# Routed results of a mixture-of-experts layer added to token rows in DRAM by indexed accumulating DMAs, in place of gathers at the end

## The reference, cut to what matters

```python
h = _rmsnorm(x, rms_weight)
logits = ht @ router_w
probs = softmax(logits)
topv, topi = top_k(probs, 2)
topv = topv / sum(topv)
eo = (silu(ht @ w_gate[e]) * (ht @ w_up[e])) @ w_down[e]
moe = sum over the two chosen e of topv * eo
sh = silu(ht @ sw_gate) * (ht @ sw_up) @ sw_down
out = x + moe + sh
```

## Time and profile before

| | |
|---|---|
| median of 3 runs | 627.8 us (627.37 to 627.97) |
| profiled execution, its own time | 628.29 us |
| its span, first to last instruction | 626.5 us |
| granted TensorE clock, mean | 0.999 |
| busy: TensorE, VectorE, ScalarE, GpSimd | 609.5, 507.5, 427.5, 192.8 us |
| instructions | 10607 |
| moved by DMA | 177.91 MB, of it q0 18.88 MB |

### The profile page before, as it was taken

One profiled execution on the slowest core, in us unless ns is written; L12 is line 12 of the kernel. 1 busy time (PEld: TensorE's weight loads), 2 busy tenths in 40 slices (PEclk: granted clock), 3 DMA queues, 4 the chain that ended last, 5 costly groups with the idle time before them and its releaser, 6 DMA issues.

```text
span 626.5 us, 10607 instructions
## 1 busy us (share of the span) xinstructions
PE 609.5 (97%) x3624; PEld 477.4 (76%) x3625; DVE 507.5 (81%) x883; ACT 427.5 (68%) x563; POOL 192.8 (31%) x174
## 2 busy tenths in 40 slices
PE   7999999998999999999999999999999999999995
PEld 6778888887887444444567888898998989889784
DVE  5888888888787787889899479788696887968687
ACT  3998888889755988888585366649385583846630
POOL 2254445425100243435940310040330404314051
PEclk9999999999999999999999999999999999999999
DMA  8977776865236997936999759695886968769357
GB/s 311 421 311 310 304 307 243 310 268 201 101 138 248 416 367 282 383 123 252 402 357 419 323 195 322 244 385 205 310 309 211 384 230 307 291 237 367 121 174 271
DMA packets 31070, 177.91 MB, mean 284 GB/s; under 512 B 4064, under 2 KB 4064, under 8 KB 14784
## 3 DMA queue, kind: packets, MB, share of 16 engines
q1 hardware_dynamic: 25536, 158.64, 66.0%
q0 software_dynamic: 5504, 18.88, 8.3%
HBM read 154.30 MB, written 23.20 MB: 283 GB/s over the span
## 4 chain that ended last, share of the span: by engine, by line
PE 69%; ACT 13%; DVE 7%; DMA 4%; issue 3%; POOL 2%; SPq 0%; DVEq 0%; POOLq 0%; ACTq 0%
PE BK L2215 11%; PE BK L307 9%; PE BK L1903 8%; PE BK L1946 6%; PE BK L2218 4%; ACT RA L1395 4%; ACT PR L1422 4%; PE BK L313 3%; PE BK L314 3%; PE BK L319 3%; PE BK L2185 3%; PE BK L2173 2%; PE BK L1848 2%; DVE WL L1038 2%; PE BK L2171 2%
## 5 line engine op out<-in xcount | busy, mean ns | idle before, releaser
L2215 PE MATMUL BK<-EX,WH 128*128 128x320 f32 x384 | 99.4, 343 | 0.0
L705 POOL TENSOR_TENSOR WL<-RC,WH 128x2048 fp32r<-128x2048 f32 x7 | 45.6, 6508 | 167.9 <-ACT WH L1603 167.9
L1038 DVE TENSOR_TENSOR WL<-RA,WH 128x2048 fp32r<-128x2048 f32 x40 | 89.3, 2288 | 9.2 <-ACT WH L1603 8.8
L2218 PE MATMUL BK<-EX,WL 128*128 128x160 f32 x336 | 79.3, 236 | 0.0
L1603 ACT ACTIVATE WH<-RA 128x2048 fp32r<-128x2048 f32 x40 | 73.7, 1908 | 0.8 <-PE BK L1946 0.8
L2215 PEld LDWEIGHTS BK<-EX,WH 128*128 128x128 f32 x384 | 69.2, 189 | 0.0
L2218 PEld LDWEIGHTS BK<-EX,WL 128*128 128x128 f32 x336 | 64.2, 191 | 0.0
L655 POOL TENSOR_TENSOR HB<-HB,ND (+2 forms) x26 | 28.6, 1120 | 100.5 <-DVE BH L922 99.8
L1712 ACT ACTIVATE HX<-SR 128x320 fp32r<-128x320 f32 x16 | 7.5, 472 | 57.0 <-DVE SR L1088 57.0
L1494 ACT ACTIVATE RA<-RA,RT 128x2048 int16<-128x2048 f32 x22 | 43.7, 1997 | 2.7 <-DVE RT L852 1.9
L1903 PE MATMUL BK<-TG,XQ 128*128 128x512 bf16 x192 | 42.4, 379 | 0.1
(11 more groups left out here) (336 smaller groups left out, 1660.9 us busy)
## 6 DMA issues: line engine op xcount, KB each, us to landing
RA<-wbit SPq DMA_DIRECT2D x54, 1024.0 KB, 6.4
RA<-wmoe SPq DMA_DIRECT2D x40, 1024.0 KB, 6.2
RC<-wmoe SPq DMA_DIRECT2D x20, 1024.0 KB, 7.8
rows<-ZERO POOLq DMA_DIRECT2D x40, 256.0 KB, 8.2
XG<-rows SPq DMA_DIRECT2D x10, 512.0 KB, 3.6
rows<-YS SPq DMA_DIRECT2D x9, 512.0 KB, 4.1
RA<-wqk SPq DMA_DIRECT2D x7, 640.0 KB, 8.1
RA<-wo SPq DMA_DIRECT2D x4, 1024.0 KB, 8.0
```

Of the source, the lines that this page charges most:

```text
L705: e.tensor_tensor(WL[2][:, at], RC[5][:, :], WH[2][:, at].bitcast(f32), ALU.subtract).then_inc(free_c[5], 1)
L1038: e.tensor_tensor(WL[m][:, q * RAW:q * RAW + RAW], RC[j][:, :], WH[m][:, q * RAW:q * RAW + RAW].bitcast(f32), ALU.subtract)\
L2215: mm = e.matmul(bank[GBK[f]][:, 0:2 * R], WH[m][:, at], EX[:, k, :, :].rearrange("p a b -> p (a b)"), start=k == 0, stop=k == KD - 1)
L2218: e.matmul(bank[GBK[f]][:, 0:R], WL[m][:, at], EX[:, k, 0, :], start=False, stop=False)
```

## The change

The results are no longer stored and gathered. SyncE copies XRES, the residual, to a new DRAM tensor `acc` (rows R to R + 511; rows 0 to R - 1 are a dump for unused rows). Each evicted routed result is multiplied by its row's weight on the way out of PSUM, and GpSimd adds it to its token's row of `acc` by an accumulating indirect DMA (`add_rows`), 128 rows of YS and 32 of YT (YT lies over the first 32 partitions of XRES's tile 0).

For this each slot needs its token and weight. GpSimd scatters such pairs (META) by SLOT to a new DRAM tensor `meta`, and SyncE loads a tile's pairs into MT (`slot_data`), for which ScalarE's and VectorE's `result` now wait (`w_in`). VectorE makes the indices IDX from them. GpSimd clears the first R rows of `acc` and all of `meta`, behind the 40 DMAs that clear `rows`. `y_st` now counts these and the accumulations; two of them must not run at once on a row, and `result(t)` and `slot_data(t)` wait for the accumulation before theirs.

At the end SyncE waits for the last accumulation, loads tiles 1 to 3 of XRES back from `acc`, copies tile 0 from `acc` straight to `out`, and VectorE only adds the shared expert's rows.

```diff
@@ sync engine
             e.wait_ge(s("zero"), 16 * NZERO)
+            e.wait_ge(s("y_st"), 32 * NS)
...
-            e.sem_inc(s("y_st"), 32 * (NS + 1))
+            e.sem_inc(s("w_in"), 32 * NS)
+            e.dma_start(MT[:, 0:2], meta_dram[0:P, :]).then_inc(s("w_in"), 16)
+            e.dma_start(MT[0:TAIL_R, 2:4], meta_dram[P:R, :]).then_inc(s("w_in"), 16)
+            e.wait_ge(s("ys_d"), NS)
+            e.dma_start(acc_dram[R:R + TOK, :].rearrange("(t p) d -> p t d", p=P), XRES[:, :, :]).then_inc(s("acc"), 16)
...
-            def store(t):
+            def slot_data(t):
                 row, tail = e.snap((t - NS) * R), e.snap((t - NS) * R + P)
-                waits(e, ("ys_a", t + 1), ("ys_d", t + 1), ("y_st", t * 32 + 32))
-                e.dma_start(rows_dram[bass.ds(row, P), :], YS[:, :]).then_inc(s("y_st"), 16)
-                e.dma_start(rows_dram[bass.ds(tail, TAIL_R), :], XY[YTAIL, :]).then_inc(s("y_st"), 16)
+                e.wait_ge(s("meta"), 1)
+                waits(e, ("y_st", t * 32))
+                e.dma_start(MT[:, 0:2], meta_dram[bass.ds(row, P), :]).then_inc(s("w_in"), 16)
+                e.dma_start(MT[0:TAIL_R, 2:4], meta_dram[bass.ds(tail, TAIL_R), :]).then_inc(s("w_in"), 16)
             def tile(t):
-                store(t)
                 e.wait_ge(s("et_pe"), t * 2 + 4)
                 e.dma_start(XG[:, :], rows_dram[bass.ds(row, P), :]).then_inc(s("e_in"), 16)
                 e.dma_start(XY[XTAIL, :], rows_dram[bass.ds(tail, TAIL_R), :]).then_inc(s("e_in"), 16)
+                slot_data(t + 1)
...
+            waits(e, ("y_st", total * 32 + 32))
+            for t in range(1, NT):
+                e.dma_start(XRES[:, t, :], acc_dram[R + t * P:R + t * P + P, :]).then_inc(s(f"acc_in{t}"), 16)
+            e.dma_start(out[0:P, :], acc_dram[R:R + P, :]).then_inc(s("out"), 16)
@@ gpsimd
+            for n in range(0, R, P // 4):
+                m = P // 4
+                e.dma_start(acc_dram[n:n + m, :].rearrange("a (u v) -> (a u) v", u=2), ZERO[0:2 * m, :])\
+                    .then_inc(s("y_st"), 16)
+            e.dma_start(meta_dram[0:GATHER, :].rearrange("(a b) c -> a (b c)", b=32), ZERO[0:GATHER // 32, 0:64])\
+                .then_inc(s("y_st"), 16)
...
+            e.wait_ge(s("meta_w"), 1)
+            for k in range(2):
+                for t in range(NT):
+                    e.indirect_dma_start(meta_dram[0:GATHER, :], bass.IndirectOffsetOnAxis(ap=SLOT[:, k, t:t + 1], axis=0),
+                                         META[:, k, t, :], None).then_inc(s("scat"), 16)
+            e.wait_ge(s("scat"), 16 * 4 * NT)
+            e.sem_inc(s("meta"), 1)
+            e.sem_inc(s("idx"), NS)
+            e.wait_ge(s("acc"), 16)
+            def add_rows(t):
+                waits(e, ("idx", t + 1), ("ys_a", t + 1), ("ys_d", t + 1))
+                e.sem_inc(s("y_new"), 1)
+                e.indirect_dma_start(acc_dram, bass.IndirectOffsetOnAxis(ap=IDX[:, 0:1], axis=0), YS[:, :], None,
+                                     compute_op=ALU.add).then_inc(s("y_st"), 16)
+                e.indirect_dma_start(acc_dram, bass.IndirectOffsetOnAxis(ap=IDX[0:TAIL_R, 1:2], axis=0), YT[:, :], None,
+                                     compute_op=ALU.add).then_inc(s("y_st"), 16)
@@ vector engine
             def result(t):
-                waits(e, ("y2_pe", t + 1), ("y_st", t * 32 + 32))
-                e.tensor_copy(YS[:, 512:1024], bank[AB[1]])
+                waits(e, ("y_st", t * 32), ("w_in", t * 32 + 32))
+                e.tensor_tensor(IDX[:, :], MT[:, 0:4:2], LANE[:, :], ALU.max).then_inc(s("idx"), 1)
+                waits(e, ("y2_pe", t + 1))
+                e.tensor_scalar(YS[:, 512:1024], bank[AB[1]], MT[:, 1:2], None, ALU.mult)
...
             e.wait_ge(s("zero"), 16 * NZERO)
+            e.wait_ge(s("y_st"), 32 * NS)
             e.tensor_copy(HE[0:8, :], bank[7][0:8, :]).then_inc(s("lgs"), 1)
...
+            e.tensor_copy(META[:, :, :, 1], WT[:, 0:2, :]).then_inc(s("meta_w"), 1)
@@ scalar engine
             def result(t):
-                waits(e, ("y2_pe", t + 1), ("y_st", t * 32 + 32), ("et_lo", t * 3 + 3))
-                e.activation(YS[:, 0:512], bank[AB[0]], ACT.Copy)
+                waits(e, ("y2_pe", t + 1), ("y_st", t * 32), ("w_in", t * 32 + 32))
+                e.activation(YS[:, 0:512], bank[AB[0]], ACT.Copy, scale=MT[:, 1:2])
...
             e.wait_ge(s("ys_d"), NS)
+            e.wait_ge(s("acc"), 16)
```

More of the change, by code:

```diff
@@ L122, in program @@
         SLOT = keep("SLOT", [P, 2, NT], i32)
+        META = keep("META", [P, 2, NT, 2], f32)
+        TOKI = keep("TOKI", [P, 2, NT], i32)
+        LANEI = keep("LANEI", [P, 2], i32)
+        LANE = keep("LANE", [P, 2], f32)
+        MT = keep("MT", [P, 4], f32)
+        IDX = keep("IDX", [P, 2], i32)
         RT = keep("RT", [P, 512], f32)
@@ L285, in program @@
                   "dself",
-                  "slots_m", "rows", "y_all", "m_hi", "e_in", "et_pe", "et_hi", "et_lo", "gate_pe", "up_pe", "gate_a", "hsum", "eh", "ht2_pe",
-                  "ht_hi", "ht_lo", "y2_pe", "ys_a", "ys_d", "y_st", "fin_in0", "fin_in1", "fin_in2", "fin_in3", "fin_b0", "fin_b1", "fin_b2", "fin_b3", "fin", "out"):
+                  "slots_m", "rows", "m_hi", "e_in", "et_pe", "et_hi", "et_lo", "gate_pe", "up_pe", "gate_a", "hsum", "eh", "ht2_pe",
+                  "ht_hi", "ht_lo", "y2_pe", "ys_a", "ys_d", "y_st", "w_in", "y_new", "meta_w", "meta", "acc", "idx", "acc_in1", "acc_in2", "acc_in3", "fin", "out"):
             s(n)
@@ L568, in _ @@
                 tile(t0 + i)
[L569 to L575, removed]
+            waits(e, ("e_in", total * 32 + 64))
+            e.sem_inc(s("y_new"), 1)
[3 more added lines that the diff above has]
+            e.dma_start(out[0:P, :], acc_dram[R:R + P, :]).then_inc(s("out"), 16)
+            waits(e, ("ys_d", total + 2))
+            e.dma_start(out[P:2 * P, :], XRES[:, 1, :]).then_inc(s("out"), 16)
+            e.wait_ge(s("fin"), 1)
+            e.dma_start(out[2 * P:3 * P, :], XRES[:, 2, :]).then_inc(s("out"), 16)
             for q in range(2):
                 cs = slice(q * 512, q * 512 + 512)
-                e.wait_ge(s("fin"), NT + q)
+                e.wait_ge(s("fin"), 2 + q)
                 e.dma_start(out[(NT - 1) * P:NT * P, cs], XRES[:, NT - 1, cs]).then_inc(s("out"), 16)
@@ L661, in _ @@
                     norm_down(t, it * 4 + t, it * (2 * GW), 2 * GW)
-            own["pool"] = Own(e, "pself")
             def newton(n):
@@ L705, in _ @@
                 e.tensor_tensor(WL[2][:, at], RC[5][:, :], WH[2][:, at].bitcast(f32), ALU.subtract).then_inc(free_c[5], 1)
-            for j in range(4):
-                e.wait_ge(free_c[j], NE + 2)
-            e.wait_ge(s("y_all"), 1)
-            for t in range(NT):
-                for k, dst in enumerate((GA, GB)):
-                    e.indirect_dma_start(dst[:, t, :], None, rows_dram[0:GATHER, :],
-                                         bass.IndirectOffsetOnAxis(ap=SLOT[:, k, t:t + 1], axis=0))\
-                        .then_inc(s(f"{('fin_in', 'fin_b')[k]}{t}"), 16)
+            group_rows(1)
+            with e.Fori(2, NE) as gi:
+                down_lo(gi)
+                group_rows(gi)
+            down_lo(NE)
+            group_rows(NE)
+            total = e.value_load(CNT[0:1, 31:32], min_val=NS + NE, max_val=MAXT)
+            add_rows(total)
         @blk.vector
@@ L1299, in _ @@
             hidden_product(total)
[L1301 to L1312 removed]
+            e.wait_ge(s("acc_in1"), 16)
             shared_result(1, total)
[L1314 removed]
             hidden_lo(total)
[L1316 to L1319 removed]
+            e.wait_ge(s("acc_in2"), 16)
             waits(e, ("y2_pe", total + 3))
@@ L1331, in _ @@
                 v = XRES[:, NT - 1, q * 512:q * 512 + 512]
-                ins = e.tensor_tensor(v, bank[2 + q], v, ALU.add)
-            o(ins)
-            e.wait_ge(s(f"fin_b{NT - 1}"), 16)
-            for q in range(2):
-                cs = slice(q * 512, q * 512 + 512)
-                e.scalar_tensor_tensor(out=XRES[:, NT - 1, cs], in0=GB[:, NT - 1, cs], scalar=WT[:, 1, NT - 1:NT],
-                                       in1=XRES[:, NT - 1, cs], op0=ALU.mult, op1=ALU.add).then_inc(s("fin"), 1)
+                e.tensor_tensor(v, bank[2 + q], v, ALU.add).then_inc(s("fin"), 1)
         @blk.scalar
@@ L2357 @@
     rows = nc.dram_tensor("rows", (DRAM_TILES * R, DM), f32, kind="Internal").ap()
-    program(nc, *args, out, rows)
+    meta = nc.dram_tensor("meta", (DRAM_TILES * R, 2), f32, kind="Internal").ap()
+    acc = nc.dram_tensor("acc", (R + TOK, DM), f32, kind="Internal").ap()
+    program(nc, *args, out, rows, meta, acc)
     r = run_bass_kernel_spmd(nc, [arrays], core_ids=[0])
```

47 lines of the change are left out of this document (20 added, 27 removed).

## The result

The changed kernel takes 651.6 us (median of 5 runs, 649.65 to 652.24) against 627.8: a ratio of 1.038, 95% interval 1.037 to 1.039. It is 23.8 us slower where I forecast 625.6 and gave a slowdown 0.16. The profiled execution is 652.24 us with a span of 650.4, against 628.29 and 626.5 before.

What follows compares the result with a forecast made beforehand. TensorE was taken as the bound, busy 609.5 of 626.5 us, except at the end, where VectorE finishes. 628.29 − 3.47 (end) + 1.25 (zeroing) = 626.07, or 625.6 us against the median; forecast range 624.9 to 626.6, overall 624.0 to 628.8.

Steps and rivals of the forecast that it cites:

- The end, gain 3.47: After TensorE's last matmuls, VectorE keeps only two additions for tile 3, ending at 620.60 instead of 624.07: 3.47 us saved.
- The small maximum for IDX (tens of elements) runs in VectorE's slack before it needs PSUM: VectorE in each routed tile: computing the indices was claimed to be covered, at no cost.
- Cost 1.25 us: Added clears behind the row buffer's 40 land at 340.7, so VectorE's logit copy, then TensorE, run 1.25 us late.
- bounds 0 to 3.3: Zeroing cost: 0 if added writes fit between others (chance 0.15), 3.3 us if each half costs a whole (0.18).
- the 0.37 MB/us of the queue alone: Clearing: rate from 2.92 MB moved in 8 us while the queue had all engines; it gives the zero-cost lower end.
- The straggler: Clearing: the late 8.2% DMA share was read as little more than one slow engine, on which the added bytes end.
- The first gather issue took 2.09 us while VectorE worked, and I take that for each: Tail: GpSimd's two accumulating issues were taken at 2.09 us each, 0.3 between, done at 599.8.
- 4.4 taken: Tail: the accumulating DMA's time to landing, taken from H3's plain scatter as 4.4 us, giving 604.2.
- 3.6 taken: Tail: one 512 KB load of XRES lands after 3.6 us, putting tile 1 at 608.2.
- rival (c): Accumulating DMA lands late; 0.2% slower from a landing of 8.8 us, 631.9 at 10.2; chance 0.15, plus 0.07 near no change.
- The rest, each 0: XRES copy to acc, pair scatters, weight prefetch, scaled evictions and removed stores and gathers: each claimed to cost 0.

Runs made afterwards that it cites:

- early_clears: Changed kernel with IDX's maximum behind the next tile's tail transposes, VectorE's tail pause, and six small clears issued near 160 us: 624.9 us, 0.996 of before.
- idx_late: Changed kernel with VectorE's maximum for IDX moved from ahead of the result evictions to behind the next tile's tail transposes: 635.6 us.
- loads_wait: Changed kernel with SyncE waiting for all clears to land before it issues group 1's weight loads: 644.4 us.
- tail_pause: Changed kernel with a pause: after the last routed result VectorE waits for GpSimd's semaphore, meant to follow both accumulating issues, before its weight splits: 647.7 us.
- early_no_pause: Changed kernel with the late IDX maximum and six small clears near 160 us, but without VectorE's wait in the tail: 627.1 us, 0.9995 of before.
- four_fixes: Changed kernel with the late IDX maximum, VectorE's tail pause, and six small clears ahead of the row buffer's: 630.8 us, 1.005 of before.

## Why the prediction was wrong, step by step

- **The end, gain 3.47: right.** early_clears shows it: TensorE's last group at 618.83, the last addition ending at 620.63 (forecast 620.60), a span 3.4 us shorter. In the changed kernel the tail gives it all back: 59.0 us from the last subtraction less the seventh maximum's 2.1 are 56.9, against 56.5 before. With the low clock taken away too, as in idx_late, it is 55.0.
- **"The small maximum for IDX (tens of elements) runs in VectorE's slack before it needs PSUM": the step that failed most.** I costed it by its elements. It was held for 4 us in each of seven tiles and made them 2.1 us longer, 14.7 us in all; idx_late gave back 16.0, with 1.9 of the tail's clock in it. The row of GpSimd's subtraction was in front of me; what I did not ask is what VectorE may do beside it. In the kernel before, behind the split that is ahead of the subtraction, every operation of VectorE in that stretch reads at most one tile in SBUF, and the change put the first other one there. None of my rivals had it.
- **"Cost 1.25 us", bounds 0 to 3.3: mis-sized.** It is a stall of 5.7 us and 7.2 in time by loads_wait; and the first subtraction is 8.8 late, beyond the upper bound too. All 8.8 are the clears: early_clears, which differs from idx_late up to there in them alone, has it at 410.6 as before, idx_late at 419.4. loads_wait has it at 412.7; of the 2.1 left there, 1.1 is a wait of TensorE for XY<-rows that the change does not have, so at least that much is a price of the late weights and not of the clears. My bytes were right but the rate was not: I took the 0.37 MB/us of the queue alone, or a few loose packets, for a stretch in which the other queue's loads fill the engines. The earlier trace rows showed q0 at 8.2%, which I read as one slow engine. The line beside it in the same view says what had the rest:

```profile
q1 hardware_dynamic: 114, 0.80, 95.1%
```

By loads_wait the 8.2% was what the other queue's loads left to q0. The straggler, on which I spent the skill's sentence, is not needed: loads_wait changed no engine, and the late landings went.
- **"The first gather issue took 2.09 us while VectorE worked, and I take that for each": wrong for the first one, 9.37.** The last landing, that of the 32 rows, was 4.93 us (4.4 taken, median 6.5 over all tiles), the load of tile 1 4.0 (3.6 taken). So rival (c), an accumulation that lands late, did happen in the tail, yet by the issue and not by the landing. Tile 1 came 9.97 us after VectorE was free.
- **"The rest, each 0": held.** No wait on MT, none on the 2 MB to acc. ScalarE's evictions with a scale take 0.68 and 0.66 us against 0.59 and 0.58, hidden.

The sum with measured terms: 628.29 − 3.4 + 14.7 + 8.8 + 3.8 (tail, from 56.9 − 56.5 + 3.4) = 652.2, and the profiled execution was 652.24. It has to come out, since its terms are the differences of the two spans at the same marks; what tests the single terms are idx_late, early_clears and tail_pause. The tail's 3.8 are 1.9 of TensorE's wait and 1.9 of its clock. Three slips of the prediction's arithmetic changed nothing: the upper bound's own landing, 342.9, gives 3.45 and not 3.3; 1.25 with 0.9 either side gives 624.7 to 626.5; and in (c) the 1.4 us are a third, not a quarter, of the way from 4.4 to 8.8.

## What to carry to other kernels

Before an instruction is added to VectorE, ask for its inputs and for what GpSimd does in those microseconds: here a two-input operation or a copy between SBUF tiles waited for the rest of a subtraction that GpSimd had started first, however small it was, and an indirect DMA issue of GpSimd waited for a whole run of VectorE's splits. A DMA added at the end of a queue is priced by what the other queue does while it drains, not by its bytes alone; one that has no need to be there costs nothing earlier. And a stall of TensorE is not priced by its length alone: the clock fell behind two of those here. A change that loses 4% can be a gain of 0.4% once three places, none of them its idea, are moved.

## What the runs showed that I had not expected

- A copy of 128x2 f32 with one SBUF input was held by GpSimd's subtraction like the two-input maximum (4.14 us).
- A GpSimd DMA issue was held over three borders between VectorE's splits, 8.8 to 9.4 us where 1.0 to 1.6 is usual, in all ten runs of the changed kernel without the pause; other issues got in at the first border.
- Five clears of 2 KB and one of 21 KB at the end of GpSimd's queue kept VectorE waiting 3.4 us; the 0.64 MB more of the full clears added 3.0.
- A wait of TensorE of under 2 us in the tail was followed by a clock of 0.56 in one run (the change) and by 1.00 in others (idx_late, early_no_pause). That made 1.9 us of difference; the pause itself was worth 2.2.
- An accumulating indirect DMA of 128 rows is issued in 1.56 us against 0.98 for a plain scatter. The median landings of the 128 and the 32 rows are 7.6 and 7.3 us in four_fixes and 5.5 and 7.1 with plain scatters on the like base, so 128 rows land some 2 us later with the add, which is no doubling; in the change they are 6.4 and 6.5.
- The pause starts VectorE's splits 1.16 us later, and TensorE's end does not move: its last group starts at 618.83 in early_clears, 618.84 before.
